# Where a graph network's first edge loop waits for its sums, and who passes on the last feature gathers of attention two

## The reference, cut to what matters

```python
# layer 0: a message network, summed over each node's edges
m_in = jnp.concatenate([h[src], h[dst], edge_attr], axis=1)
m = jax.nn.relu(m_in @ eW1 + eb1) @ eW2 + eb2
agg = segment_sum(m, dst)                      # then an update network on [h, agg]
# layer 2 (attention two): 8 heads of 32
key_j = k[src] + (edge_attr @ We + be)
alpha = softmax over ALL edges of (q[dst] * key_j).sum(-1) / sqrt(32)
out = segment_sum(v[src] * alpha, dst) + bias
```

## Time and profile before

| | |
|---|---|
| median of 3 runs | 3915.79 us (3914.08 to 3916.58) |
| the profiled execution's own time | 3911.31 us |
| its span, first to last instruction | 3909.5 us |
| granted TensorE clock, mean | 0.839 of full speed |
| loop one, first L1393 to last sum | 560.8 to 1283.5 us |
| attention two, first to last L2052 | 2480.8 to 3100.4 us |

### The profile page before, as it was taken

One profiled execution on the slowest core, in us unless ns is written; L12 is line 12 of the kernel. 1 busy time (PEld: TensorE's weight loads), 2 busy tenths in 40 slices (PEclk: granted clock), 3 DMA queues, 4 the chain that ended last, 5 costly groups with the idle time before them and its releaser, 6 DMA issues. The chain is left out here.

```text
span 3909.5 us, 59454 instructions
## 1 busy us (share of the span) xinstructions
PE 2789.2 (71%) x13639; PEld 1620.7 (41%) x13639; DVE 2932.6 (75%) x6788; ACT 940.4 (24%) x2734; POOL 2590.5 (66%) x2675
## 2 busy tenths in 40 slices
PE   5446789999998899699999977799999640000007
PEld 4345432333332688456666544466665320000004
DVE  7897548888887333299999966699999666666664
ACT  0011112222221233245545522222222120000004
POOL 0487567777766577677777756677777337777772
PEclk8555699999999899799999988899999865555559
DMA  4487447777776333377777732688787424444440
GB/s 199 131 262 241 113 125 211 212 213 210 207 205 166 81 68 70 90 211 212 211 211 212 204 79 72 193 238 237 238 239 226 103 70 108 108 108 108 108 103 34
DMA packets 430094, 629.44 MB, mean 161 GB/s; under 512 B 254381, under 2 KB 290834, under 8 KB 428832
## 3 DMA queue, kind: packets, MB, share of 16 engines
q0 software_dynamic: 168064, 505.00, 45.4%
q1 hardware_dynamic: 252608, 94.37, 9.7%
q10 hardware_dynamic: 9312, 28.71, 2.3%
HBM read 549.09 MB, written 78.40 MB: 161 GB/s over the span
## 5 line engine op out<-in xcount | busy, mean ns | idle before, releaser
L1291 POOL DMA_INDIRECT edge_ring<-tab,edge_rec x480 | 468.5, 976 | 179.1 <-issue 133.4
L2350 POOL DMA_INDIRECT state<-tab,edge_rec x480 | 453.9, 946 | 157.1 <-issue 145.9
L1976 PE MATMUL edge_psS<-edge_terms,ident 128*128 128x256 f32 x1952 | 472.1, 385 | 19.0 <-DVE edge_psS L2020 18.8
L2522 PE MATMUL gate_psT<-ident,gate_hb 128*128 128x128 f32 x50 | 9.9, 286 | 612.0 <-ACT gate_hb L2483 612.0
L1976 PEld LDWEIGHTS edge_psS<-edge_terms,ident 128*128 128x128 f32 x1952 | 361.0, 192 | 202.6 <-DVE edge_psS L2020 152.3
L1857 POOL DMA_INDIRECT state<-tab,edge_rec x360 | 340.5, 946 | 122.7 <-issue 105.1
L1857 POOL DMA_INDIRECT state<-tab,edge_feat x360 | 340.5, 946 | 121.4 <-issue 106.4
L1358 PE MATMUL edge_psX<-state,ident 128*128 x720 | 375.2, 630 | 38.7 <-DVE edge_ring L1393 38.6
L1995 PE MATMUL edge_psX<-state,ident 128*128 128x512 f32 x720 | 350.7, 611 | 18.4 <-DMA state<-tab,edge_feat 16.8
L1393 DVE TENSOR_TENSOR edge_ring<-edge_psX,edge_ring 128x1024 f32<-128x1024 f32 x240 | 294.0, 1225 | 74.8 <-PE edge_psX L1370 27.1
L2052 DVE TENSOR_TENSOR edge_prod<-edge_psX,state 128x1024 f32<-128x1024 f32 x240 | 293.9, 1225 | 17.3 <-PE edge_psX L1995 13.9
(11 more groups left out here) (499 smaller groups left out, 6104.1 us busy)
## 6 DMA issues: line engine op xcount, KB each, us to landing
sorted_d<-state SPq DMA_DIRECT2D x8, 2312.0 KB
feat_d<-state SPq DMA_DIRECT2D x32, 528.0 KB, 5.7
edge_feat<-sorted_d SPq DMA_DIRECT2D x116, 136.0 KB
edge_feat<-feat_d SPq DMA_DIRECT2D x113, 132.0 KB
state<-tab,edge_rec POOLq DMA_INDIRECT x840
state<-src_rows ACTq DMA_DIRECT2D x26, 512.0 KB
state<-low_rows ACTq DMA_DIRECT2D x26, 512.0 KB
edge_ring<-tab,edge_rec POOLq DMA_INDIRECT x600
```

The lines of the kernel that those rows point to most:

```text
L1291: pool.indirect_dma_start(out=ring[:, k, s, :], out_offset=None, in_=S["tab0"][:, :], in_offset=bass.IndirectOffsetOnAxis(ap=rec[:, k, R_S ...
L1976: last = pe.matmul(so_far, S["ident"][:, :], terms[:, s, :], start=False, stop=(s == QE - 1), skip_group_check=True)
L2350: pool.indirect_dma_start(out=ring[:, k, s, :], out_offset=None, in_=S["tab3"][:, :], in_offset=bass.IndirectOffsetOnAxis(ap=rec[:, k, R_S ...
```

## The change

In loop one the wait for a sum's completion moves from right behind each sum to where the sum is read: between sums 0 and 1 and between 2 and 3 it stays; that for sum 1 stands ahead of sum 2, behind the step's second L1393; that for sum 3 stands behind the next step's first L1393, ahead of the no-op that releases the buffer, or at the turn's end. In attention two `pass_on` goes from SyncE; in the far turn GpSimd itself waits for the feature gather ahead of the rows of its step, increments `s_feat`, and goes on to the rows.

```diff
@@ -1383,7 +1383,7 @@
                 head.load(rec[0:1, 0, R_BLOCK:R_BLOCK + 1])
                 with nc.Fori(0, n, engines=[dve.engine], hint_back_edge=True) as t:
                     step = Chain(dve, s_v, t * CH)
-                    b_next = head.value()
+                    b_next, summed = head.value(), 0
                     for q in range(AQ):
                         k, b = q % RING_0, b_next
                         for h in range(2):
@@ -1392,17 +1392,24 @@
                             dve.wait_ge(s_x, t * (2 * AQ) + (2 * q + h + 1))
                             dve.tensor_tensor(both, psX[:, 2 * h:2 * h + 2, :], both, ALU.add).then_inc(s_xr, 1)
                             if h == 0 and q:
+                                step.until(summed)
                                 dve.nop().then_inc(s_done[(q - 1) % RING_0], 1)
                             if h and q < AQ - 1:
                                 b_next = block_of(dve, t, q + 1)
                             elif h:
                                 hold(dve, s_rec[0], uses(t, AQ, RING_0) * 16)
                                 head.load(rec[0:1, 0, R_BLOCK:R_BLOCK + 1])
+                            if h:
+                                step.until(summed)
+                                dve.nop(nofuse=True)
                             dve.wait_ge(s_xr, t * (2 * AQ) + (2 * q + h + 3))
                             for s in (2 * h, 2 * h + 1):
                                 to = blk(S["big"], b) if s == QE - 1 else psS[:, :]
                                 so_far = psS[:, :] if s else blk(S["big"], b)
-                                step(dve.scalar_tensor_tensor(to, ring[:, k, s, :], 0.0, so_far, ALU.max, ALU.add))
+                                if s % 2:
+                                    step.until(summed)
+                                summed = step.put(dve.scalar_tensor_tensor(to, ring[:, k, s, :], 0.0, so_far, ALU.max, ALU.add))
+                    step.until(summed)
                     dve.nop().then_inc(s_done[k], 1)
         ph.close()
 
@@ -1820,10 +1827,6 @@
                     sp.dma_start(feat[:, q % RING, :, :].rearrange("p s f -> p (s f)"),
                                  steps_of[:, bass.ds(at, 1), :].rearrange("p a f -> p (a f)")).then_inc(s_feat[q % RING], 16)
 
-                def pass_on(t, q):
-                    hold(sp, s_far[q % RING], uses(t, q, RING) * 16)
-                    sp.nop().then_inc(s_feat[q % RING], 16)
-
                 n = turns(sp)
                 if layer == 1:
                     with nc.Fori(0, n, engines=[sp.engine], hint_back_edge=True) as t:
@@ -1841,7 +1844,6 @@
                     with nc.Fori(0, far_turns(sp), engines=[sp.engine], hint_back_edge=True) as t:
                         for q in range(AQ):
                             load(t + m, q, (t + begin) * AQ + q)
-                            pass_on(t, q)
                     for q in range(AHEAD):
                         load(n, q, q)
                         load_near(q, q)
@@ -1882,7 +1884,8 @@
                                     far_features(t, t + m, a)
                             if q + TURNED < AQ:
                                 far_features(t, t + m, q + TURNED)
-                            hold(pool, s_feat[q % RING], uses(t + m, q, RING) * 16)
+                            hold(pool, s_far[q % RING], uses(t, q, RING) * 16)
+                            pool.nop().then_inc(s_feat[q % RING], 16)
                             rows(q % RING)
 
             @block.scalar
```

## The result

| | before | changed |
|---|---|---|
| median of 4 runs | 3915.81 us (3914.08 to 3916.58) | 3884.80 us (3883.12 to 3890.64) |
| ratio | | 0.9922, 95% [0.991, 0.9934] |
| the profiled execution's own time | 3911.31 us | 3890.64 us |
| its span | 3909.5 us | 3888.9 us |

The account below looks back on a forecast made before the run. VectorE was taken to pace loop one, with GpSimd right behind, and a chain of hand-offs attention two's last turn. Gains of 15.1 + 15.0 = 30 us off 3915.8 gave 3886, range 3877 to 3902.

Parts of the forecast that it names:

- part 1: Loop one's sums: moving 15 waits a turn off VectorE's path saves 15.1 us, ends 10 and 21.
- part 2: Attention two's last turn: GpSimd handing over the feature gathers instead of SyncE saves 15.0 us, ends 9 and 18.
- The gap behind a sum: Loop one, sums 1 and 3 to L1393: gap goes from 0.13 to -0.01 us, 0.14 saved per place.
- The moved waits: Loop one, behind L1393: waits placed there cost nothing; without cover 0.12 us at up to 15 places, 1.8 a turn.
- Row turns held by GpSimd: Loop one's 11 turns with scatters: GpSimd bounds at 46.28 us a turn; 8.8 us gained by step 88 (5.9 to 11.8).
- The landing term: Loop one, step 88: its row gathers take 5.8 us to land, the middle of 2.8 and 8.7.
- Turns 11 to 13: Loop one's turns without scatters: VectorE sets the pace again, gaining 3 x 2.1 = 6.3 us (4.0 to 9.5).
- The last turn: Loop one's turn gathering features through SyncE: VectorE does not set its pace, so it moves as a whole.
- (a): Rival: loop one's waits cost nothing, or moved ones cost what removed ones did; only part 2 counts, 3901; chance 0.08.
- (b): Rival: GpSimd's hand-over comes late for ScalarE, attention two's turn end stays; part 1 alone, 3901; chance 0.08.
- (c): Rival: in both places some remaining wait ends at the same time; no change, 3916; chance 0.04.
- (d): Rival: in loop one's steps 24 to 88 PE idles and its clock falls; slower, 3947; chance 0.04.

Follow-up runs that it names:

- e3: Kernel before, with VectorE still waiting for sums 1 and 3 ahead of each L1393, but behind the other checks: 3909.16 us against 3914.38.
- e4: Changed kernel with four groups of scatters (16) moved from loop one to the later projection stage: 3873.11 us against 3914.47 for the kernel before.
- e5: Kernel before the change with the same four groups of scatters moved to the projection stage: 3913.15 us against 3914.47.
- e6: Changed kernel, but in attention two's last turn SyncE hands over again, loading records two steps ahead: 3887.84 us against 3914.38 for the kernel before.
- e1: Kernel before with only loop one's waits for sums moved, attention two as before: 3901.93 us against 3914.38.
- e2: Kernel before with only attention two's hand-over moved from SyncE to GpSimd, loop one as before: 3899.55 us against 3914.38.
- e7: Changed kernel, with GpSimd also handing over the gathered features in loop one's last turn: 3879.20 us against 3914.47 for the kernel before.
- e11: e7 with four scatter groups moved to the projection and the degrees' store issued before loop one's last turn: 3870.15 us against 3914.95 for the kernel before.

## Why the prediction was right, and where its terms were off

The direction was right, and so was the mechanism of part 1 and of part 2 up to the last hand-overs. That the total was right to 1 us (3886 for 3884.8) is luck: the sizes inside were off both ways and made up for each other, as part 1 gave 11.4 for 15.1 and part 2 gave 17.1 for 15.0.

**The gap behind a sum.** Taken at -0.01, between the ends -0.08 and 0.04; it is -0.09 and -0.08, the end set by the pair that overlaps and a hair past it. The held no-op on which I argued for the middle costs nothing when it is queued ahead of time. So a place is worth 0.22, not 0.14, and a turn without scatters takes 43.3 instead of 44.8, a gain of 3.5 (15 x 0.22 = 3.3 of it). e3 shows why the middle was wrong: I had held the 0.13 for the price of a wait, but 0.10 of it is what stood behind the wait.

**The moved waits** were costed at nothing, rightly: L1393 to sum 0 and to sum 2 are still 0.15 and 0.03.

**Row turns held by GpSimd.** The bound was named rightly, and e4 against e5 shows it. Its size was not: 46.77 a turn instead of 46.28. My step took a turn of before in which GpSimd was not held, and that was a fair one: the ten turns of before, less 3.5 us of waits, come to 46.26 each. But it held the issue time for fixed, and it isn't; the page's entry for the gathers, before and then changed (columns after the count: busy us, mean ns of one, idle before it):

```profile
L1291 POOL DMA_INDIRECT edge_ring<-tab,edge_rec x480 | 468.5, 976 | 179.1 <-issue 133.4
```

```profile
L1291 POOL DMA_INDIRECT edge_ring<-tab,edge_rec x480 | 476.0, 992 | 160.8 <-issue 136.2
```

These are means over the whole loop. Over turns 1 to 10 alone the 320 gathers took 313.2 us and now take 317.2, 0.4 a turn, and a wait of 1.6 us for a record in turn 1 does the rest, so GpSimd starts turn 11 5 us later than my sum had it. What makes an issue longer stands in the timelines of VectorE and GpSimd:

```profile
1098.11 0.70 DVE L1411 SCALAR_TENSOR_TENSOR edge_psS<-edge_ring,state 128x512 f32<-128x512 f32 x1 [0.15 <-DVE edge_ring L1393]
1098.37 1.24 POOL L1291 DMA_INDIRECT edge_ring<-tab,edge_rec  x1 [0.30 <-issue]
```

The gather begins while sum 0 runs and ends 0.81 behind that sum's end. Of the changed kernel's 480 gathers 74 take longer than 0.98 us; all but one begin inside a sum 0, the only one of the four that reads two tensors from SBUF, and each of these 73 ends 0.81 to 0.84 behind that sum. The 321 that begin inside one of the other three sums or an L1393 take 0.95 on average, 0.97 at most. In the kernel before 59 gathers begin inside a sum 0, in the changed one 91, and the time above 0.945 a gather grows from 14.9 to 22.4 us, the 16 ns of the means. So sum 0 holds the issue until it is over, and the new pace of VectorE makes the two meet more often. The landing term errs the other way: from the end of a step's last gather issue to the L1393 that uses it there are 4.8 us at the start of seven of the nine turns 2 to 10, where I had taken 5.8; this gives 1.0 back. The sum, 8.8 - 5.1 + 1.0 = 4.7, is the 4.5 measured at step 88. This is the term that was most off, 8.8 for 4.5.

**Turns 11 to 13** were to give 6.3 and gave 7.7: 3.5, 3.5 and 0.7. In turn 13 one wait of L1393 for PE takes 4.1 us, where before the longest was 1.9. I had let the faster pace run on to the far turn, and the hand-over of its features doesn't follow. ScalarE's list has the condense of step 113 ahead of the copy of 112's transposes, on which PE waits:

```profile
1212.36 0.42 ACT L1320 ACTIVATE edge_dense<-edge_feat 128x256 f32<-128x256 f32 x1 [7.88 <-SPq L1003]
```

The first L1393 of step 112 starts 2.3 us behind it, at 1214.67; it did so before, too (2.3), and in e4 (2.5). The gather of 113's features is issued 9.9 us behind that of 112 in the change and 6.5 in e4, where turn 13 takes 43.32: so it is not PE's own pace that holds turn 13. Why that gather is late is open. With a step of 5.30 against PE's own 5.27 nothing more is to be had from VectorE elsewhere. The last turn moved as a whole but for 0.6.

**Part 2.** The last gather of rows comes 15.0 earlier, for 14.8 forecast, and up to step 111 nothing is gained, near the forecast, which had it up to 113. The last product gains 17.1, since from the end of that gather's issue to the product there are now 8.5 us, where I carried over the 10.6 of before. The step that failed is that ScalarE's increments come with the rows of each step. In GpSimd's list the increment for step 113 stands behind the rows of 112 and the features of 115, the latter issued at 3030.00; yet ScalarE condenses 113 at 3026.82, released by it. The same at the end: condense of 117 starts 573.9 and of 119 582.1 behind the first product, while the gathers that stand ahead of those increments are issued until just before the rows of 117 and 119, which start at 579.3 and 589.3. The hand-over runs some 4 to 7 us ahead of the gathers around it, so it does not set the end. e6 agrees: there SyncE hands over as the gathers land, condense of 119 starts 580.9 behind the first product, and the last product comes no earlier, at 603.0. What PE still waits for in the last three steps of the change is rows: 0.47, 1.63 and 0.83 us.

**The rivals.** (a) fell with the gaps and with e1, 12.5 us in its median and 11.3 in its loop. The rule behind it, from the Trainium skill, page "VectorE: DVE Perf Modes", section "The DRAIN you can't avoid", is that the pipeline drains after each operation and that a semaphore adds nothing. The same section says that a next operation that is not held starts earlier, which my prediction left out; the -0.09 agrees with that sentence, and no run here agrees that a semaphore adds nothing. The same two instructions stand 0.13, 0.03 or -0.09 apart, by whether the second waits for the first and what is queued behind the wait. (b) fell with e2, 17.0 us in its loop. (c) fell with both. (d) didn't come. In the page's slices of 97 us steps 24 to 88 of the loop lie in the eighth to the twelfth, and PE's clock stands at 9 there, as before:

```profile
PEclk8555699999999899799999989899999865555559
```

Left open: whether a sum 0 of another form would free GpSimd. The mean issue is 967 to 976 ns in the three kernels with the old sums (before, e2, e5), where 45 to 59 gathers begin inside a sum 0, and 992 to 999 in the ten with VectorE packed closer, where 85 to 103 do. The traces show which gathers are held and until when; that the two SBUF inputs of sum 0 are the reason is argued from its being the only sum with two, and no run changed that.

## What to carry to other kernels

When two engines are within a per cent or two of each other, saving on the first brings only the distance to the second: look for work of the second that can go to a stage where it idles, measure how much idle there is (here 22 us, which one move used up), and move it in the same change: moved alone, it left the time as it was (e5). Keep a wait for completion only where its result is read, and where it must stay, put it behind the checks that are passed already. In a queue that both loads and hands over, issue the loads ahead of the hold that they don't depend on.

## What the runs showed of the hardware that I had not expected

- VectorE starts an instruction 0.08 to 0.09 us ahead of the end of the one before when nothing waits, 0.03 behind it when the wait stands last, and 0.13 behind it when two passed checks and a held no-op stand behind the wait (change, e3, before).
- An increment in GpSimd's list is carried out while gathers that stand ahead of it are still to be issued: some 4 to 7 us ahead in the changed kernel's last turn of attention two.
- One store of single floats delays the landing of gathers beside it: a feature gather by some 10 us in e7, rows by 6.6 in e11. The stretch it stood in was longer by 7.4, 9.8 and 12.7 us in the three places tried.
- GpSimd's issue of an indirect gather isn't a constant. It takes 0.945 us, but one that begins while VectorE's sum 0 runs ends 0.81 behind that sum's end, up to 1.47 us in the changed kernel: 73 of 480 gathers, on the engine that bounds those turns.
